# A routed expert network after two attention layers: register loads placed earlier, a transposing DMA for row transposes, one affine for a sum

## The reference

```python
x = x + gate_layer(layernorm(x))                  # stage A
x = x + retention(layernorm(x), ctx, ctx)         # stage B
u = layernorm(x)                                  # the third layer, _L0_ffn_ref(u)
xn = rms_norm(u, norm_scale)
scores = einsum('bsd,ed->bse', xn, w_router)
_, ids = top_k(scores, 2)
c = take_along_axis(softmax(scores), ids)
val, gate = split(einsum('bsd,ehd->bseh', xn, w_up), 2)
y = einsum('bseh,edh->bsed', val * silu(gate), w_down)
out = sum(y[ids] * c, axis=2) + u                 # u is the skip
x = x + out
```

## Time and profile before

| what | value |
|---|---|
| median of three runs | 457.16 us |
| the profiled execution | 458.88 us |
| its span, first to last instruction | 457.1 us |
| PE busy | 380.0 us (83%) |
| DVE busy | 275.5 us (60%) |
| ACT busy | 258.8 us (57%) |
| POOL busy | 199.6 us (44%) |
| mean granted clock of TensorE | 0.931 |

### The profile page before, as it was taken

How to read it: one execution, slowest core, us unless ns; L and a number is a source line. 1 busy time by engine, 2 the same in 40 slices (tenths; PEclk the granted TensorE clock), 3 DMA queues, 4 the chain that set the end, 5 groups by cost and what they waited for, 6 DMA issues and landing times.

```text
span 457.1 us, 10128 instructions
## 1 busy us (share of the span) xinstructions
PE 380.0 (83%) x2600; PEld 272.5 (60%) x2601; DVE 275.5 (60%) x688; ACT 258.8 (57%) x473; POOL 199.6 (44%) x186
## 2 busy tenths in 40 slices
PE   1899997899885211499999999999999999999980
PEld 0687786787774211256666666666666666666650
DVE  3789787979797999554444444454444444444440
ACT  2799786776775631555445545554555555554530
POOL 2634637668788403224343334343443344333221
PEclk9999998999998555599999999999999999999996
DMA  7999850622221240112222222222222322223220
GB/s 248 408 426 403 288 184 1 204 73 70 69 93 62 77 142 1 36 29 45 48 36 36 45 47 35 44 39 47 43 37 37 47 47 35 36 45 45 26 25 11
DMA packets 24645, 41.93 MB, mean 92 GB/s; under 512 B 5040, under 2 KB 20400, under 8 KB 23600
## 3 DMA queue, kind: packets, MB, share of 16 engines
q1 hardware_dynamic: 17088, 31.17, 19.1%
q0 software_dynamic: 7536, 10.52, 14.3%
HBM read 32.17 MB, written 9.50 MB: 91 GB/s over the span
## 4 chain that ended last, share of the span: by engine, by line
PE 67%; DVE 13%; ACT 8%; issue 5%; POOL 2%; DMA 2%; SPq 1%; ACTq 0%; DVEq 0%; POOLq 0%
PE bank L1220 30%; PE bank L1241 6%; PE bank L1270 5%; PE bank L1271 5%; PE bank L1272 5%; ACT arena L434 4%; DVE expert_w L842 3%; PE bank L1107 2%; PE bank L1155 2%; PE bank L1252 2%; DVE expert_w L833 2%; ACT arena L449 2%; PE bank L1164 2%; PE bank L1060 1%; DVE arena L988 1%
## 5 line engine op out<-in xcount | busy, mean ns | idle before, releaser
L1220 PE MATMUL bank<-expert_w,arena 128*128 x702 | 159.2, 364 | 4.4 <-ACT arena L617 4.4
L732 POOL DMA_INDIRECT out<-arena,add_idx x39 | 61.7, 1581 | 114.8 <-ACT arena L598 114.8
L1220 PEld LDWEIGHTS bank<-expert_w,arena 128*128 128x128 f16 x702 | 65.8, 98 | 54.2 <-issue 6.8
L1037 DVE SCALAR_TENSOR_TENSOR arena<-bank,dn_small,arena 128x512 f32<-128x512 f32 x78 | 45.3, 581 | 38.2 <-PE bank L1220 23.4
L722 POOL DMA_INDIRECT arena<-xrow_hbm,take_idx x39 | 38.7, 994 | 58.1 <-PE bank L1252 43.3
L1270 PE MATMUL bank<-expert_w,arena 128*128 x195 | 53.1, 273 | 0.9 <-DVE arena L1021 0.9
L1271 PE MATMUL bank<-expert_w,arena 128*128 x195 | 53.2, 273 | 0.0
L1272 PE MATMUL bank<-expert_w,arena 128*128 x195 | 53.1, 273 | 0.0
L1021 DVE COPY arena<-bank 128x1024 f16<-128x1024 f16 x39 | 27.0, 692 | 37.8 <-PE bank L1241 37.8
L617 ACT ACTIVATE arena<-bank 128x512 f16<-128x512 f16 x39 | 23.3, 597 | 37.1 <-PE bank L1252 37.1
L1043 DVE TENSOR_TENSOR arena<-arena 128x512 f16<-128x512 f32 x39 | 27.0, 692 | 27.1 <-ACT arena L623 27.1
(11 more groups left out here) (179 smaller groups left out, 736.5 us busy)
## 6 DMA issues: line engine op xcount, KB each, us to landing
expert_w<-in_wup SPq DMA_DIRECT2D x8, 1408.0 KB, 17.2
expert_w<-in_wdn SPq DMA_DIRECT2D x10, 640.0 KB, 4.7
rows<-in_x SPq DMA_DIRECT2D x8, 256.0 KB, 6.3
arena<-in_ctxT SPq DMA_DIRECT2D x8, 256.0 KB, 3.2
xrow_hbm<-front SPq DMA_DIRECT2D x8, 256.0 KB, 2.2
out<-rows SPq DMA_DIRECT2D x8, 256.0 KB, 2.7
expert_w<-in_wdn SPq DMA_DIRECT2D x20, 64.0 KB, 4.9
cst_b<-in_consts_b SPq DMA_DIRECT2D x1, 960.0 KB, 13.6
```

Source lines behind the costliest of these rows:

```text
L732: pool.indirect_dma_start(out=out, in_=yt[:, i % 2], in_offset=None, out_offset=bass.IndirectOffsetOnAxis(ap=add_idx[:, i:i + 1], axis=0), ...
L1037: V.scalar_tensor_tensor(out=hh[:, cols], in0=src, scalar=h_scale[:, ds(e, 1)], in1=sg[:, cols], op0=ALU.mult, op1=ALU.mult).then_inc(s_h, 1)
L1220: last = T.matmul(bank[q][:, 0:n], xsT[:, slot, (2 * a + c) * P:(2 * a + c + 1) * P], up_w[:, ds(w0 + c * UPC + w * 2 * H + lo, n)], start ...
```

## The change

**Slot loop, expert numbers.** VectorE's two loads stand at the start of a step, ahead of L1021's wait. ScalarE's load stands ahead of its wait for y. TensorE's load for the down product stands between the third and fourth matmul of the second up part; in the looped steps the load for the up product of a k = 1 step stands in the down product of the step before, after six of its matmuls, and that of a k = 0 step stays where it was.

**Slot loop, rows.** SP issues a transposing DMA for each slot, from `xs` to `xsT`. It waits for the gathered rows and for the third up part of two slots before. The transposes of TensorE and the copy of ScalarE are gone. GpSimd gathers four slots ahead instead of five and waits for the transposing DMA of two slots before instead of TensorE's transposes.

**Stage B, x2 plus its layernorm.** x2 + (x2·s + b) is computed as x2·(1 + s) + b: GpSimd adds 1 to the scale (a tiny instruction between L698 and L701), and ScalarE writes the rows in place, after L559 and L509 and ahead of L570. L523 on ScalarE and L690 on GpSimd are gone.

```diff
@@ SP @@
+            for i in range(NSLOT):
+                sp.wait_ge(s_xs[i % 2], 16 * (i // 2) + 16)
+                if i >= 2:
+                    sp.wait_ge(s_up, 3 * i - 3)
+                sp.dma_start_transpose(xsT[:, i % 2], xs[:, i % 2, 0:4 * P]).then_inc(s_xsT[i % 2], 16)
@@ ScalarE, stage B @@
-                if live(r, 3, NBATCH):
-                    b, _, slot = at(it, k, 3)
-                    act.wait_ge(s_r34, b + 1)
-                    if r >= 4:
-                        act.wait_ge(s_x2s, b)
-                    for j in range(2):
-                        last = nc.scalar.activation(sk[:, j], rows[:, ds(b * 2 + j, 1), :].squeeze(1), ACT.Identity,
-                                                    bias=nb3[:, slot, j:j + 1], scale=r34[:, slot, 0, j:j + 1])
-                    last.then_inc(s_s, 1)
...
                     if r < NBATCH + 2:
                         xn_high(b)
+                    act.wait_ge(s_r34, b + 1)
+                    act.wait_ge(s_xn, b + 1)
+                    for j in range(2):
+                        row = rows[:, ds(b * 2 + j, 1), :].squeeze(1)
+                        last = nc.scalar.activation(row, row, ACT.Identity, bias=nb3[:, slot, j:j + 1],
+                                                    scale=ve3[:, slot, 0, j:j + 1])
+                    last.then_inc(s_x2s, 1)
@@ ScalarE, slot loop @@
+                if live(r, 1, NSLOT):
+                    i, _, _ = at(it, k, 1)
+                    e = act.snap(act.value_load(tile_e[0:1, ds(i, 1)], min_val=0, max_val=NE - 1))
                 if live(r, 3, NSLOT):
...
-                    act.wait_ge(s_trx, i + 1)
-                    if r >= 2:
-                        act.wait_ge(s_up, 3 * i - 3)
-                    nc.scalar.activation(xsT[:, slot], rowsT_bank, ACT.Copy).then_inc(s_xsT, 1)
@@ GpSimd @@
-                    pool.wait_ge(s_s, b + 1)
-                    pool.wait_ge(s_xn, b + 1)
-                    nc.gpsimd.tensor_tensor(rows[:, ds(b * 2, 2), :], sk, rows[:, ds(b * 2, 2), :], ALU.add).then_inc(s_x2s, 1)
...
+                    nc.gpsimd.tensor_tensor(ve3[:, slot, 0], r34[:, slot, 0], const("ones")[:, 0:2], ALU.add)
...
-                    pool.wait_ge(s_trx, i - 1)
+                    pool.wait_ge(s_xsT[i % 2], 16 * (i // 2))
...
-            for i in range(5):
+            for i in range(4):
                 take(i)
...
-                if i + 5 < NSLOT:
-                    take(i + 5)
+                if i + 4 < NSLOT:
+                    take(i + 4)
@@ TensorE, slot loop @@
+            def up(i, slot, w0, q, lo, n, between=None):
                 for m, (c, a, w) in enumerate(products):
+                    if m == 3 and between:
+                        between()
...
+                    if k == 0 or r < 4:
+                        load_expert("up", i, 2 * UPC)
...
-                    up(i, slot, w_up, 1, HA, HA)
-                if live(r, 0, NSLOT):
-                    i, half, slot = at(it, k, 0)
-                    pe.wait_ge(s_xs[slot], 16 * half + 16)
-                    if r >= 1:
-                        pe.wait_ge(s_xsT, i)
-                    for n in range(4):
-                        last = T.transpose(rowsT_bank[:, n * P:(n + 1) * P], xs[:, slot, n * P:(n + 1) * P], ident16[:, :])
-                    last.then_inc(s_trx, 1)
+                    up(i, slot, w_up, 1, HA, HA, load_down_expert if live(r, 2, NSLOT) else None)
...
                     for c in range(NH - 1):
+                        if c == 2 and k == 0 and 4 <= r < NSLOT:
+                            load_expert("up", at(it, k, 0)[0], 2 * UPC)
```

More of the change, by code:

```diff
@@ L554, in step_b @@
                 if live(r, 3, NBATCH):
-                    b, _, _ = at(it, k, 3)
+                    b, _, slot = at(it, k, 3)
                     act.wait_ge(s_tr3, b + 1)
@@ L1036, in step_e @@
                             dve.wait_ge(s_hlo, 2 * i + q - 1)
[L1037 removed]
+                        V.scalar_tensor_tensor(out=hh[:, cols], in0=src, scalar=h_scale[:, ds(e_h, 1)], in1=sg[:, cols],
                                                op0=ALU.mult, op1=ALU.mult).then_inc(s_h, 1)
@@ L1225, in step_e, with load_down_expert @@
             def step_e(it, k, r):
+                def load_down_expert():
+                    load_expert("down", at(it, k, 2)[0], 2 * DNC)
                 if live(r, 1, NSLOT):
-                    i, _, slot = at(it, k, 1)
-                    w_up = pe.snap(pe.value_load(tile_e[0:1, ds(i, 1)], min_val=0, max_val=NE - 1) * (2 * UPC))
-                    pe.wait_ge(s_xsT, i + 1)
+                    i, half, slot = at(it, k, 1)
+                    if k == 0 or r < 4:
+                        load_expert("up", i, 2 * UPC)
+                    w_up = expert["up"]
+                    pe.wait_ge(s_xsT[slot], 16 * half + 16)
                     if r >= 2:
@@ L1260, in step_e @@
                     i, _, _ = at(it, k, 2)
-                    w_dn = pe.snap(pe.value_load(tile_e[0:1, ds(i, 1)], min_val=0, max_val=NE - 1) * (2 * DNC))
+                    if not live(r, 1, NSLOT):
+                        load_expert("down", i, 2 * DNC)
+                    w_dn = expert["down"]
                     if r == 2:
```

28 lines of the change are left out of this document (14 added, 14 removed).

## The result

The changed kernel takes 440.98 us (median of four runs, 438.92 to 442.36) against 457.35 for the kernel before beside it: 0.9639 of its time, 95% interval 0.9593 to 0.9686. Forecast: 439.9, range 436 to 447.5. Run again later, it took 439.85 (439.37 to 443.99, six runs) against 457.69, 0.9628 [0.9595, 0.9662]. Its profiled execution took 439.83 us, span 438.0; that of before had 457.1.

The account below looks back on a forecast made before the run. TensorE, waiting 0.21 us per looped step on VectorE's register loads, was taken to bound the slot loop; −11.3 − 1.0 − 0.9 − 0.4 − 1.2 − 2.5 = −17.3 us gave 439.9 from the median 457.16, range 436 to 447.5.

Parts of the forecast that it names:

- The step that carried the forecast: Slot loop: 29 looped steps fall from 6.47 to 6.08 us as VectorE's loads and TensorE's row transposes go, −11.3 us.
- The 0.04 for loads between matmuls: Slot loop, second up product: TensorE's moved register load shows as 0.04 us a step, between nothing and 0.40.
- VectorE's margin: Slot loop: VectorE's own cycle becomes 5.90 us, below TensorE's step of 6.04, 6.08 with gaps.
- The transfer: Slot loop: the transposing DMA takes T = 3.7 us from issue to landing, like a plain load of its size.
- The rival of the late transfer: Ahead of the first up product: the transposing DMA stalls TensorE from T = 6.1, slower than before from about 7; 12%.
- The first two steps: Slot loop's entry, ahead of the written-out steps: two more row transposes fall away, −0.4 us.
- The sum, −2.5: Stage ahead of routing, x2 as one affine: −2.9 + 0.8 − 0.4 = −2.5 us, bounds −4 and +2.
- The second step: Stage ahead of routing, first step with L523: without it VectorE's L901 follows L890 at 77.54 instead of 79.75, −2.2.
- The contention: Stage ahead of routing: VectorE's L842 took 2.00 instead of 1.03 beside POOL's big add, which goes; 0.4 us credited.
- VectorE's loads did not bind: Rival in the slot loop: VectorE's cycle with both loads sets a step of about 6.2 us, 443.4 us total; 13%.
- the load inside the up product did not show: Rival in the slot loop: TensorE's load shows, 6.44 us a step, 450.3 total, or half the gap, 444.5; 10%.
- the wait had no other cause: Rival: the wait before the h transposes (L1241) has another cause, so moved loads do nothing, 446.1 us; 3%.

Follow-up runs that it names:

- e4: Kernel before with only VectorE's two register loads moved ahead of its wait for the h transposes: 449.63 us, 0.9834.
- e3: Kernel before with only the row transposes moved to a transposing DMA, register loads and x2 as before: 454.75 us, 0.9949.
- e5: Changed kernel with TensorE's register loads back at the start of the first up product and of the down product: 440.79 us, 0.9637.
- parts 1 and 2: Expert numbers loaded ahead of the waits (1), row transposes by DMA (2), against the kernel before: alone 5.7 and 2.5 us gained, together 441.63 us.
- e8: Changed kernel with a third register load on VectorE ahead of its wait for the h transposes: 450.08 us (one run).
- e7: Changed kernel with POOL gathering three slots ahead instead of four: 574.52 us (one run).
- e12: Changed kernel with TensorE's loads at old places, late x2 affine, and 12 unread 128x512 products on TensorE ahead of the slot loop: 436.56 us, 0.9556.
- e6: Changed kernel with the x2 affine moved to the end of ScalarE's step in the last two steps that have it: 437.99 us, 0.9584.
- e11: Changed kernel with x2 as in the kernel before, loads moved and row transposes by DMA kept: 441.63 us, 0.9645.
- e9: Changed kernel unedited, run again: 439.85 us.

## Why the prediction was right, point by point

**The bound and the loop.** The step that carried the forecast held. VectorE's two loads were the cause of the 0.21 us (e4: 6.258 a step), the row transposes the other 0.22, and their sum came only with both: taken alone, the DMA gave the loop nothing (e3), since VectorE's cycle of 6.47 stood over it. With the transposes gone and TensorE's loads at their old places (e5) the step is 6.036, 0.222 under e4's 6.258. The working reads this rightly, as a change of who is late; adding the parts' own results would have given 8.2 for parts 1 and 2 where 16.1 came.

**The 0.04 for loads between matmuls** was right in size and wrong in place. In the second up product, where I feared a gap, the matmuls lost nothing: in five of the steps the weight load behind the register load came 0.16 to 0.22 us late, and these steps took 6.03 to 6.05 like the others. The gaps are in the down product, at the up product's load, in six of the looped steps, and are gone with the loads at their old places (e5). My ground, that loads between matmuls are hidden everywhere in the trace, went too far: the loads of the trace stood behind matmuls of 0.215 us or a whole product of them, this one behind six of 0.11. That the shorter matmuls are the reason was not tried, and alone they cannot be, since ten of the sixteen loads at that place left no gap.

**VectorE's margin** was mis-sized. I had 5.90 against 6.04; e8 gives about 5.6. I priced both loads at their full 1.10 and 1.05 and laid them end to end behind L1045; a load behind another costs 0.7, and part of both lies beside L1043, L1044 and the h transposes.

**The transfer.** T was mis-sized: I took 3.7, measured are 2.56 from issue to landing at the entry and 2.65 to the product in e7. The 128 KB load out of HBM was the wrong nearest row, the gather's 2.8 the better one. By the Trainium skill's "VectorE: DVE Perf Modes", section "The three transpose paths", four blocks would have made 5.2 (an estimate, four times its 1309 ns); the trace does not bear that out. (The advice for TensorE that the prediction gives beside this figure stands in that page's section "Rules for kernel authors".) The Trainium skill's "Advanced Engine Details and Errata", section "X-Bar Transpose (TRN2)", has such a DMA as fast as a plain one, and the traces agree: 2.4 us median landing in e3 and e7, where the plain loads of 128 KB took 3.5 to 3.9. The entry gained 2.29 instead of 1.2. The chain around it I had as 6.1 + T; the changed kernel's rows give 6.3 to 6.8 + T, so a stall would have begun at T near 5.3 to 5.9, not 6.1. The rival of the late transfer was somewhat nearer than I held it, though T was half of what it needed.

**The first two steps** were to gain 0.4 and gained nothing: with an earlier first product, more of the two steps runs at half clock. I had left the clock out of the entry; e12 shows that it was worth 1 to 1.5 us.

**Stage B.** The sum, −2.5, is what the undisturbed traces give (−2.4). Its terms were not. The second step gave 0.0 to 0.8, not 2.2; the third 1.14, not 0.7; and at the end of the stage, where I had allowed 0.4 of gain and 0.8 of loss, the time from the last scores to VectorE's first copy of the down weights (L842, now L836) fell from 13.3 to 14.4 us to 12.45, and 0.6 went back to the affine in ScalarE's way. The contention that I read from L842's 2.00 us went as forecast: none of the sixteen in the changed kernel takes over 1.02. Errors of both signs met, so that the sum came out is luck.

**The rivals.** VectorE's loads did not bind, the load inside the up product did not show, and the wait had no other cause. The sum was worked out on an execution that stood 1.7 us above the median and was then set against the median. Its half-clock step in stage B cost 1.3 us (13.38 against 12.09); that this makes up most of the 1.7 is likely, not shown.

**The total.** 17.3 us were forecast; 16.4 and 17.8 were measured in the two comparisons. The loop's 11.3 was foreseen by its mechanism. The rest came out near because the entry gave more, the first two steps less, and the terms of stage B cancelled.

## What to carry to other kernels

Where two engines take turns at being late, give each edit its price only after asking who is late without it: in this loop one edit was worth nothing alone and nearly half of the gain in company. A register load cost VectorE 1.05 us between short instructions here and about 0.7 behind another load, so it belongs ahead of a wait that is sure to be long, and not between short instructions. When an engine's row of work starts earlier after an idle stretch, ask at which clock it starts.

## What the runs showed of the hardware

- A transposing DMA of 128x512 fp16 within SBUF took 1.19 us of SP's time to issue and 2.4 us in the median from issue to landing (up to 3.1 in e3, where scatter, gather and these transfers kept the DMA engines busy for 0.36 of the time).
- A third register load on VectorE, behind two others, added about 0.7 us (e8); single ones between short instructions took 1.05 (kernel before).
- Steps of stage B that fell to half clock in one profiled execution and not in another took 1.3 (before), 1.4 (e6) and 3.2 us (e5) longer (1.06 against 0.60 us for two 128x256 products). In the kernel before TensorE had waited 1.92 us ahead of such rows, where e11 had 1.26 and kept full clock; in e5 and e6 it had waited no longer than in e9 and e12, which kept it. What decides stays open.
- Twelve products of 128x512 (4.92 us) ahead of the slot loop brought the granted clock from 0.50 to 1.00 at its entry.
